# The experts' end of a decoder: results read back in portions by rank, summed in eight banks, normed in place

## The chip, the cores and the metric

The program is a small two-layer decoder in one kernel on one core of a Trainium2 chip. The metric is device time in microseconds (us), the median of the runs of one comparison. For the kernel before these are 3485.11 us, the median of three runs (3482.16 to 3487.38).

## The reference

The decoder runs three blocks twice, each with a residual and a layer norm. Only the last block matters here, a mixture of 64 experts with 8 of them for each of 2048 rows:

```python
x = _layernorm(x + _L1_ffn_ref(x, gate_w, w_gate, w_up, w_down), axis=-1)      # last line of the model
# inside _L1_ffn_ref: E = 64 experts, TOP_K = 8, HIDDEN = 256, FFN = 96, C = 2*N*8/64 = 512 slots an expert
scores, idx = top_k(softmax(x @ gate_w.T), 8)
xbuf = zeros((E, C, D)).at[e_sorted, pos].set(x[tok_sorted], mode='drop')
y = einsum('ecf,edf->ecd', silu(g) * u, w_down)
y_pair = y[e_sorted, safe_pos] * (s_sorted * valid)
out = zeros((N, D)).at[tok_sorted].add(y_pair)
```

So every output row is the row itself plus eight results of experts, each times its weight, and then a layer norm over 256 values.

## The kernel before

The stages run one after the other; the last is `stage_moe`. Its first part (`stage_cross`) writes each row to the slots of its experts in the DRAM table `xbuf` and keeps in `rows.row` (SBUF) the row itself, and a running count by which an expert knows its rank within a row's eight. Ranks go by expert number: rank 0 is the chosen expert with the lowest number, rank 7 the one with the highest. The second part, which the change touches, is the one block under `m = Mem(nc, ctx, "exp")`.

**The loop over pairs.** `PAIRS` is 32: two experts a pair, `i` from 0 to 31. SP loads the slots of both (`inputs`, L1442, three pairs deep) and the weights (`upper` L1377, `lower` L1382). PE turns the rows over (L1489), multiplies for gate (L1503) and up (L1507), and for the results `y` (L1520). ACT copies half of the turned rows (L1542), computes silu (L1553) and copies the results out of PSUM into the arena (L1563). DVE copies the other half (L1592), makes the addresses `cur` (L1596) and the products `h` (L1610, L1613). In every second pair, `i % 2`, DVE also makes the eight weights of one tile of 128 rows: three operations (L1621, L1624, L1627), 16 tiles in all. GpSimd (POOL) sends the results: four indirect DMAs an expert (L1662), 256 in all, each scattering up to 128 rows of 1 KB to `ytok` in DRAM, where row r and rank k lie at row 8r + k. Empty slots are skipped. After the sends of an expert it waits until those of the third expert back have landed, and frees their buffers.

**The end.** When all sends have landed, SP loads the results by tile: `load(t)` (L1465) brings all eight ranks of 128 rows, 8 KB in one piece for each partition, 1 MB a tile, into one of seven slots. Six slots lie in the arena that held inputs and results of the loop. Further loads wait until a slot is free. For each tile DVE adds ranks 0 and 1 times their weights to the row (L1641, `SCALED = 2`); ACT makes six diagonal matrices (L1571) and PE multiplies ranks 2 to 7 by them into one PSUM bank of four (L1533); DVE adds the bank (L1648) and takes mean and variance (L76, L79, L80); POOL makes the reciprocal root and the shift (L87, L90, L1676); ACT writes the normed tile into one of four buffers `out` (L1583); SP stores it (L1476). `RING = 4` buffers of each kind go round, so that diagonals wait for sums, sums for norms, and ACT's output for the store of four tiles before. Loads and stores are on SP's one queue, in the order in which they are issued.

Of the kernel before, what the change touches and what calls it, by code (L numbers as in the profile page):

```python
# [14 lines left out]
ALU = mybir.AluOpType  # L15
# [3 lines left out]
P = 128  # L19
# [1338 lines left out]
def stage_moe(nc, xc, dst, hold, qd, kd, xbuf, ytok, A):  # L1358
# [6 lines left out]
    with ExitStack() as outer:  # L1365
# [27 lines left out]
        with ExitStack() as ctx:  # L1393
# [3 lines left out]
            SLOTS, RING, SCALED = 7, 4, 2  # L1397
            TURNED = K - SCALED
            XG, Y, LOAD = QB * WIDTH, QB * D, K * D
# [7 lines left out]
            spare = m.sb("spare", [P, K, D])  # L1407
            yg = [cut(u * LOAD, LOAD, D) for u in range(SLOTS - 1)] + [spare[:, :, :]]
            part, out = ([m.sb(f"{n}{u}", [P, D]) for u in range(RING)] for n in ("part", "out"))
            diag = [m.sb(f"diag{u}", [P, TURNED, P]) for u in range(RING)]  # L1410
            power, eps = m.sb("power", [P, 1]), m.sb("eps", [P, 1])
            waiter, var, rstd, shift = ([m.sb(f"{n}{u}", [P, 1]) for u in range(RING)] for n in ("waiter", "var", "rstd", "shift"))
            st, mv = [m.sb(f"st{u}", [P, 6]) for u in range(RING)], [m.sb(f"mv{u}", [P, 2]) for u in range(RING)]
# [4 lines left out]
            same, same_w = m.sb("same", [P, K, E]), m.sb("same_w", [P, K, E])  # L1418
# [12 lines left out]
            y_in, stored, summed = m.sems("y_in", SLOTS), m.sems("stored", RING), m.sems("summed", RING)  # L1431
            diag_ready, sum_filled, shift_ready, norm_consts = m.sem("diag_ready"), m.sem("sum_filled"), m.sem("shift_ready"), m.sem("norm_consts")
            ln = [NormSems(m, u) for u in range(RING)]

            Mem.clear(nc)
            with nc.Block() as block:
                @block.sync
                def _(sp):
# [21 lines left out]
                    for b in range(RESULTS):  # L1460
                        for s in S:
                            sp.wait_ge(sent[b][s], len(range(b, PAIRS, RESULTS)) * QB * 16)

                    def load(t):
                        sp.dma_start(yg[t % SLOTS], results[:, t, :, :]).then_inc(y_in[t % SLOTS], 16)  # L1465

                    for t in range(SLOTS):
                        load(t)
                    for t in range(TILES + 2):
                        if t + SLOTS < TILES:  # L1470
                            sp.wait_ge(ln[t % RING].r, t // RING + 1)
                            load(t + SLOTS)
                        if t >= 2:
                            u = (t - 2) % RING
                            sp.wait_ge(ln[u].out, (t - 2) // RING + 1)
                            sp.dma_start(dst[(t - 2) * P:(t - 1) * P, :], out[u][:, :]).then_inc(stored[u], 16)  # L1476
                    for u in range(RING):
                        sp.wait_ge(stored[u], len(range(u, TILES, RING)) * 16)

                @block.tensor  # L1480
                def _(pe):
# [12 lines left out]
                    for i in range(PAIRS):  # L1494
# [18 lines left out]
                        for s in S:  # L1513
                            pe.wait_ge(h_ready[s], i + 1)
                            pe.wait_ge(late_ready[s], i + 1)
                            if i + 1 < PAIRS:
                                pe.wait_ge(x0_ready[s], i + 2)
                                pe.wait_ge(x1_ready[s], i + 2)
                            for b in range(QB):
                                last = pe.matmul(pxy[s][b // 2][:, b % 2 * D:b % 2 * D + D], h[s][:, b * P:b * P + P], wd[i % 2][s][:, :],  # L1520
                                                 start=True, stop=True)
                            last.then_inc(y_filled[s], 1)
                    for t in range(TILES):
                        u = t % RING
                        total = pxy[u // 2][u % 2]
                        pe.wait_ge(diag_ready, t + 1)
                        if t < RING:
                            pe.wait_ge(y_ready[u // 2], PAIRS)
                        else:
                            pe.wait_ge(ln[u].r, t // RING)  # L1530
                        pe.wait_ge(y_in[t % SLOTS], t // SLOTS * 16 + 16)
                        for k in range(TURNED):
                            last = pe.matmul(total[:, 0:D], diag[u][:, k, :], yg[t % SLOTS][:, SCALED + k, :], start=k == 0, stop=k == TURNED - 1)  # L1533
                        last.then_inc(sum_filled, 1)

                @block.scalar
                def _(act):
                    def half(i, s):
                        act.wait_ge(x_filled[s], i + 1)
                        if i:  # L1540
                            act.wait_ge(u_filled, i)
                        act.copy(xgT[s][:, 1, :], pxy[s][1][:, :]).then_inc(x1_ready[s], 1)  # L1542

                    for s in S:
                        half(0, s)
                    for i in range(PAIRS):
# [19 lines left out]
                    def diagonals(t):  # L1566
                        act.wait_ge(weight_ready, t + 1)
                        if t >= RING:
                            act.wait_ge(sum_filled, t - RING + 1)
                        for k in range(TURNED):  # L1570
                            last = act.mul(diag[t % RING][:, k, :], ident[:, :], weight[:, t, SCALED + k:SCALED + k + 1])  # L1571
                        last.then_inc(diag_ready, 1)

                    for t in range(RING):
                        diagonals(t)
                    for t in range(TILES):
                        u = t % RING
                        if t + RING < TILES:
                            diagonals(t + RING)
                        act.wait_ge(shift_ready, t + 1)  # L1580
                        if t // RING * 16 > 0:
                            act.wait_ge(stored[u], t // RING * 16)
                        act.activation(out[u][:, :], part[u][:, :], ACT.Identity, bias=shift[u][:, :], scale=rstd[u][:, :])\  # L1583
                           .then_inc(ln[u].out, 1)

                @block.vector
                def _(dve):
# [15 lines left out]
                    for i in range(PAIRS):  # L1603
# [12 lines left out]
                        if i % 2:  # L1616
                            t, done = i // 2, i // 2
# [6 lines left out]
                            dve.tensor_tensor(same_w[:, :, :], same[:, :, :], rows.weight[:, t:t + 1, :].broadcast_to([P, K, E]), ALU.mult)\  # L1624
                               .then_inc(same_w_ready, 1)
                            dve.wait_ge(same_w_ready, done + 1)
                            dve.tensor_reduce(weight[:, t, :], same_w[:, :, :], AX.X, ALU.add).then_inc(weight_ready, 1)  # L1627

                    dve.wait_ge(weight_ready, TILES)
                    for first in range(0, TILES, 2):  # L1630
                        tiles = first, first + 1
                        for k in range(SCALED):
                            for t in tiles:
                                u, turn = t % RING, t // RING
                                if k:
                                    dve.wait_ge(summed[u], turn * SCALED + k)
                                else:
                                    dve.wait_ge(y_in[t % SLOTS], t // SLOTS * 16 + 16)
                                    if turn > 0:
                                        dve.wait_ge(ln[u].out, turn)  # L1640
                                dve.scalar_tensor_tensor(out=part[u][:, :], in0=yg[t % SLOTS][:, k, :], scalar=weight[:, t, k:k + 1],  # L1641
                                                         in1=part[u][:, :] if k else rows.row[:, t, 0:D], op0=ALU.mult, op1=ALU.add)\
                                   .then_inc(summed[u], 1)
                        for t in tiles:
                            u, turn = t % RING, t // RING
                            dve.wait_ge(sum_filled, t + 1)
                            dve.wait_ge(summed[u], turn * SCALED + SCALED)
                            dve.tensor_tensor(part[u][:, :], part[u][:, :], pxy[u // 2][u % 2][:, 0:D], ALU.add).then_inc(ln[u].r, 1)  # L1648
                        for t in tiles:
                            u = t % RING  # L1650
                            norm_stats(dve, ln[u], [part[u][:, :]], [st[u][:, :]], [mv[u][:, :]], waiter[u], t // RING, 1)

                @block.gpsimd
                def _(pool):
# [15 lines left out]
                    for t in range(TILES):  # L1670
                        u = t % RING
                        if t >= RING:
                            pool.wait_ge(ln[u].out, t // RING)
                        norm_rstd(pool, ln[u], [mv[u][:, :]], [var[u][:, :]], eps[:, :], power[:, :], [rstd[u][:, :]], t // RING, 1)
                        pool.wait_ge(ln[u].rstd, t // RING + 1)
                        pool.tensor_scalar(shift[u][:, :], mv[u][:, 0:1], rstd[u][:, 0:1], -1.0, ALU.mult, ALU.mult).then_inc(shift_ready, 1)  # L1676
# [1301 lines left out]
```

## Time and profile before

| | |
|---|---|
| runs | 3485.11, 3487.38, 3482.16 us (median 3485.11) |
| profiled execution | 3484.81 us, of which the trace's span is 3483.1 us |
| mean granted TensorE clock | 0.968 of full speed |
| busy share of the span | PE 93%, weight loads 65%, DVE 68%, ACT 56%, POOL 59% |
| HBM read and written | 162.39 MB and 125.83 MB |

Times in rows are microseconds from the start of the span, unless marked ns. "Idle before" is how long the engine had nothing to do before the instruction, and the name behind the arrow is what ended that. A clock of 1.00 is 2.4 GHz, 0.50 is 1.2 GHz. The DMA share is the mean busy share of the core's 16 DMA engines.

### The profile page before, as it was taken

The page shows a single profiled execution, that of the slowest core. Times are in us where ns is not written, and L with a number is a line of the kernel's source. Part 1 is how long each engine was busy: PE and PEld are TensorE (multiplying, and loading weights), DVE is VectorE, ACT ScalarE, POOL GpSimd, SP SyncE. Part 2 cuts the span into 40 slices and gives each one's busy share as a digit, 9 for nine tenths or more (in the row PEclk, how much of TensorE's full clock was granted, in tenths as well). Part 3 has the DMA queues.
Part 4 walks back from the last instruction along what each step waited for, and adds up shares of the span by engine and source line. Part 5 has one row for each costly group of instructions (what it writes and reads, how often), then busy time and mean ns, then how long its engine had stood idle before and what let it go on. Part 6 is the DMA issues. An engine that isn't in the chain of part 4 may idle for free. (4 is left out here: it accounts for less than half of the span.)

```text
span 3483.1 us, 96172 instructions
## 1 busy us (share of the span) xinstructions
PE 3252.1 (93%) x37284; PEld 2271.6 (65%) x37284; DVE 2369.0 (68%) x4702; ACT 1952.6 (56%) x5231; POOL 2061.5 (59%) x3037
## 2 busy tenths in 40 slices
PE   9999899887899999999999999999999899699996
PEld 6777566465577777777777777777776455356665
DVE  5555477434677878787777878787777688444443
ACT  1111366422577677666777677767776477445555
POOL 3333477642566666666666666666666467657774
PEclk9999799997899999999999999999999899899998
DMA  2000555001111111111111111111210466266655
GB/s 86 17 11 12 134 130 121 30 1 25 53 55 58 46 51 51 52 43 52 49 52 55 40 51 54 52 43 51 60 40 21 109 162 173 104 224 209 213 181 232
DMA packets 222970, 278.87 MB, mean 80 GB/s; under 512 B 58420, under 2 KB 187000, under 8 KB 215832
## 3 DMA queue, kind: packets, MB, share of 16 engines
q1 hardware_dynamic: 201212, 236.71, 24.0%
q0 software_dynamic: 18432, 34.96, 2.9%
q8 instruction: 300, 4.92, 0.6%
q10 hardware_dynamic: 2876, 1.06, 0.1%
q14 instruction: 150, 1.23, 0.1%
HBM read 162.39 MB, written 125.83 MB: 83 GB/s over the span
## 5 line engine op out<-in xcount | busy, mean ns | idle before, releaser
L2333 PE MATMUL head_ring<-gd_xT,head_w 128*128 128x512 f32 x1024 | 508.6, 620 | 9.2 <-DMA head_w<-gd_w 6.8
L1662 POOL DMA_INDIRECT ytok<-exp_arena,exp_cur x256 | 251.0, 981 | 118.0 <-issue 73.5
L2661 DVE TENSOR_TENSOR head_Xs<-head_bx,head_join 128x512 bf16<-128x512 f32 x320 | 219.9, 687 | 80.9 <-PE head_bx L2375 80.9
L2333 PEld LDWEIGHTS head_ring<-gd_xT,head_w 128*128 128x128 f32 x1024 | 175.5, 191 | 148.6 <-issue 135.4
L2626 DVE SCALAR_TENSOR_TENSOR head_cb_V<-head_ring,head_taps,head_cb_V 128x504 f32<-128x504 f32 (+2 forms) x384 | 263.1, 727 | 2.8 <-ACT head_cb_V L2488 2.8
L2458 PE MATMUL head_by<-head_wo,head_ogT 128*128 128x256 f32 x1016 | 254.0, 393 | 7.0 <-issue 0.3
L2342 PE MATMUL head_ring<-head_w,gd_xT 128*128 128x256 f32 x1024 | 258.6, 396 | 0.0
L2458 PEld LDWEIGHTS head_by<-head_wo,head_ogT 128*128 128x128 f32 x1016 | 183.2, 190 | 37.3 <-DVE rows_xc L2694 13.7
L2342 PEld LDWEIGHTS head_ring<-head_w,gd_xT 128*128 128x128 f32 x1024 | 186.0, 191 | 32.4 <-issue 0.3
L2533 ACT CAST head_Tt<-head_btt 128x512 bf16<-128x512 f32 x320 | 194.3, 607 | 17.7 <-PE head_btt L2383 15.9
L2553 ACT COPY head_U<-head_bu 128x512 f32<-128x512 f32 x256 | 137.4, 589 | 109.8 <-PE head_bu L2421 109.8
L2626 DVE SCALAR_TENSOR_TENSOR head_cb_Q<-head_ring,head_taps,head_cb_Q 128x504 f32<-128x504 f32 (+2 forms) x192 | 141.0, 734 | 60.2 <-ACT head_cb_Q L2488 55.6
L1224 DVE TENSOR_REDUCE cf_top<-cf_near 128x4 f32<-128x1024 f32 x128 | 154.9, 1220 | 33.0 <-PE cf_near L1054 32.8
L2666 DVE TENSOR_TENSOR head_rest<-head_V,head_br 128x512 bf16<-128x512 f32 x128 | 88.0, 688 | 123.0 <-PE head_by L2439 117.9
L2530 ACT CAST head_Ti<-head_bx 128x512 bf16<-128x512 f32 x256 | 152.2, 595 | 34.2 <-PE head_bx L2293 34.2
L1146 ACT ACTIVATE cf_prob<-cf_score 128x512 f32<-128x512 f32 x256 | 145.7, 601 | 40.4 <-PE cf_score L1068 37.4
L749 ACT ACTIVATE cb_prob<-cb_score 128x384 f32<-128x384 f32 x256 | 121.6, 491 | 65.8 <-PE cb_score L682 63.5
L1610 DVE TENSOR_TENSOR exp_h<-exp_pgu,exp_act_g 32x512 f32<-32x512 f32 x64 | 44.2, 690 | 166.0 <-ACT exp_act_g L1553 166.0
L2560 ACT ACTIVATE head_o<-head_bu 128x128 f32<-128x128 f32 x512 | 137.5, 299 | 33.3 <-PE head_bu L2439 33.3
L1354 POOL DMA_INDIRECT xbuf<-moe_row,cf_to x128 | 127.0, 992 | 46.3 <-issue 38.7
L2755 POOL TENSOR_TENSOR head_knrm<-head_sums,gd_eps 128x4 f32<-128x4 f32 x64 | 13.3, 208 | 237.3 <-ACT head_kq L2516 237.3
L309 PE MATMUL la_bank<-la_xT,hold_place 128*128 128x256 f32 x640 | 149.1, 388 | 3.0 <-ACT la_xT L367 2.0
(389 smaller groups left out, 9342.9 us busy)
## 6 DMA issues: line engine op xcount, KB each, us to landing
xbuf<-head_blank SPq DMA_DIRECT2D x64, 552.0 KB
exp_arena<-xbuf SPq DMA_DIRECT2D x64, 552.0 KB, 5.2
hold_place<-scan SPq DMA_DIRECT2D x64, 256.0 KB, 4.6
ytok<-head_blank SPq DMA_DIRECT2D x64, 256.0 KB
exp_arena<-ytok SPq DMA_DIRECT2D x14, 1024.0 KB, 12.4
moe_w<-moe_w SPq DMA_DIRECT2D x32, 384.0 KB, 3.1
hold_place<-qd SPq DMA_DIRECT2D x48, 192.0 KB
hold_place<-kd SPq DMA_DIRECT2D x48, 192.0 KB
```

The costliest lines, as they stand in the source:

```text
L309: last = pe.matmul(b[:, j * N:j * N + N], wqk[:, c, h * DH:h * DH + DH], xT[u][:, c, :], start=c == 0, stop=c == DC - 1)
L1146: act.activation(prob[n % RING][:, :, :].rearrange("p i k -> p (i k)"), score[n % 2][:, :], ACT.Exp, scale=SCALE)\
L1224: dve.tensor_reduce(top[t % 2][:, :, j:j + 3:2].rearrange("p i j -> p j i"), near[n // 2 % 2][:, :].rearrange("p (a i k) -> p a i k", a=2, ...
L1662: pool.indirect_dma_start(ytok, bass.IndirectOffsetOnAxis(ap=cur[i % AHEAD][s][:, b:b + 1], axis=0), y[i % RESULTS][s][:, b, :], None, bou ...
L2333: last = pe.matmul(b[:, :], w[:, c, FEAT[what]], xT[:, c, n % UNITS * N:n % UNITS * N + N], start=c == 0, stop=c == DC - 1)
L2342: last = pe.matmul(b[:, i * D:i * D + D], xT[:, c, rows], w[:, c, FEAT["Z"]], start=c == 0, stop=c == DC - 1)
L2458: last = pe.matmul(bank[:, i * D:i * D + D], ogT[:, i, 2 * h + f, :], wo[:, h, :], start=h == 0, stop=h == REP - 1)
L2530: act.copy(Ti[:, :, :].rearrange("p q i -> p (q i)"), bt[:, :]).then_inc(t_ready, 1)
L2533: act.copy(Tt[:, :, :].rearrange("p q i -> p (q i)"), btt[:, :]).then_inc(tt_ready, 1)
L2560: last = act.activation(o2[:, v, block * P:block * P + P], bu[v][:, block * P:block * P + P], ACT.Square, accum_out=oss[:, v, block:block ...
L2626: dve.scalar_tensor_tensor(out=out, in0=by_seq(bank_of(f, n))[:, :, 0:SEQ - s], scalar=taps[:, TAP[f], KS - 1 - s:KS - s], in1=out, op0=AL ...
L2661: dve.tensor_tensor((Ti if a == 0 else Xs)[:, :, :], bx[:, :].rearrange("p (q i) -> p q i", i=SEQ), join[:, a, :].unsqueeze(1).broadcast_t ...
```

## The change

All of it is in the second part of `stage_moe`; the loop's matmuls, copies and sends are left as they are.

1. The results are read back in four portions by rank: portion g holds ranks 2g and 2g + 1 of all 16 tiles, 4 MB, in pieces of 2 KB (2 KB out of each 8 KB). SP issues portion g when the sends of pair 28 + g have landed (`results_sent` also waits for the two pairs before). Portion 0 lies in `hold.place`, portion 1 in `xc`, portion 2 in the arena (it also waits until the last inputs and addresses are read), portion 3 again in `hold.place`, for which it waits until DVE has added ranks 0 and 1 of all tiles. Portions 0 and 1 are two DMAs each, portion 2 four, portion 3 eight (one for two tiles).
2. DVE makes the weights of one tile in each pair from 1 to 16, in place in `hold.place`.
3. All 80 diagonals have a place of their own. ACT makes three of them in each pair from the fifth on, between its copies of turned rows and of results.
4. DVE adds ranks 0, 1 and 2, straight into `rows.row`, rank after rank over all 16 tiles. PE sums ranks 3 to 7 in eight banks, two tiles a bank: first rank 3 of all tiles, then ranks 4 and 5 of tiles 0 to 7, then for each bank ranks 6 and 7, with ranks 4 and 5 of tiles 8 to 15 in between.
5. Bank by bank DVE adds the sum and takes the statistics of two tiles, POOL makes roots for both at once, ACT norms `rows.row` in place, and SP stores from there. No buffer is waited for.

```diff
-            SLOTS, RING, SCALED = 7, 4, 2
+            ALONE = 3
+            TURNED, HALF = K - ALONE, K // 4
+            yg = [[hold.place[:, t * LOAD:t * LOAD + LOAD] for t in range(TILES)], [xc[:, t, :, :].rearrange("p k d -> p (k d)") for t in range(TILES)],
+                  [arena[:, t * LOAD:t * LOAD + LOAD] for t in range(TILES)],
+                  [hold.place[:, t * LOAD:t * LOAD + LOAD] for t in range(TILES)]]
+            diag = m.sb("diag", [P, TILES * TURNED, P])
+            totals = [m.ps("total"), pgu[0], pgu[1], pu, pxy[0][0], pxy[0][1], pxy[1][0], pxy[1][1]]
...
-                    for t in range(SLOTS):
-                        load(t)
-                    for t in range(TILES + 2):
-                        if t + SLOTS < TILES:
-                            sp.wait_ge(ln[t % RING].r, t // RING + 1)
-                            load(t + SLOTS)
+                    def results_sent(pair):
+                        for i in range(pair, -1, -1)[:RESULTS]:
+                            for s in S:
+                                sp.wait_ge(sent[i % RESULTS][s], (i // RESULTS + 1) * QB * 16)
+                    sp.wait_ge(weight_ready, TILES)
+                    for g in range(len(LOADS)):
+                        results_sent(PAIRS - len(LOADS) + g)
+                        if g == 2:
+                            for s in S:
+                                sp.wait_ge(x_filled[s], PAIRS)
+                                sp.wait_ge(cur_ready[s], PAIRS)
+                        if g == 3:
+                            sp.wait_ge(summed, 2 * TILES)
+                        for i, (first, last, to) in enumerate(LOADS[g]):
+                            sp.dma_start(to, results[:, first:last, g * HALF:g * HALF + HALF, :]).then_inc(y_in[g][i], 16)
+                    for t in range(TILES):
+                        sp.wait_ge(ln.out, t + 1)
+                        sp.dma_start(dst[t * P:t * P + P, :], row[t]).then_inc(stored, 16)
...
+                    def term(t, k):
+                        total = totals[t // 2][:, t % 2 * D:t % 2 * D + D]
+                        g = k // HALF
+                        pe.wait_ge(diag_ready, t * TURNED + k - ALONE + 1)
+                        pe.wait_ge(y_in[g][load_of(t, k)], 16)
+                        return pe.matmul(total, diag[:, t * TURNED + k - ALONE, :], value(t, k), ...)
+                    for t in range(TILES // 2):
+                        middle(t)
+                    for t in range(0, TILES, 2):
+                        for a in range(t, t + 2):
+                            for k in range(3 * HALF, K):
+                                last = term(a, k)
                         last.then_inc(sum_filled, 1)
+                        if t < TILES // 2:
+                            middle(TILES // 2 + t)
+                            middle(TILES // 2 + t + 1)
...
+                        diagonals((i - 4) * 3)
...
-                        if i % 2:
-                            t, done = i // 2, i // 2
+                        if 0 < i <= TILES:
+                            t, done = i - 1, i - 1
...
+                    for k in range(ALONE):
+                        for t in range(TILES):
+                            dve.scalar_tensor_tensor(out=row[t], in0=value(t, k), scalar=weight[:, t, k:k + 1], in1=row[t], op0=ALU.mult, op1=ALU.add)\
+                               .then_inc(summed, 1)
+                    for b in range(TILES // 2):
+                        tiles = 2 * b, 2 * b + 1
+                        dve.wait_ge(sum_filled, b + 1)
+                        for t in tiles:
+                            dve.tensor_tensor(row[t], row[t], totals[b][:, t % 2 * D:t % 2 * D + D], ALU.add).then_inc(ln.r, 1)
+                        norm_stats(dve, ln, [row[t] for t in tiles], [st[:, t, :] for t in tiles], [mv[:, t, :] for t in tiles],
+                                   waiter[:, 2 * b:2 * b + 2], b, 2)
```

## Rows read from the trace of the kernel before

**Rows 1.** Windows: start:end, length, busy time by engine, clock, DMA share, GB/s.

```profile
3165.00:3176.00 11.00, 10.89 (x48) 6.69 (x48) 6.36 (x12) 5.67 (x11) 7.92 (x9) 1.00 0.67 214
...
3420.00:3430.00 10.00, 3.13 (x8) 2.53 (x9) 1.27 (x3) 0.00 (x0) 0.40 (x1) 0.50 0.74 284
...
3440.00:3450.00 10.00, 10.00 (x48) 8.81 (x47) 6.33 (x24) 6.45 (x21) 5.33 (x12) 1.00 1.01 425
```

**Rows 2.** Chain that ended last, from 3419 us: start, length, what.

```profile
3419.42 2.28 DMA ytok<-exp_arena,exp_cur
...
3421.91 4.83 DMA exp_arena<-ytok
...
3445.68 13.21 DMA out<-exp_out
...
3476.28 0.60 ACT exp_out L1583
```

**Rows 3.** Timeline of GpSimd in the last pairs: sends of the results.

```profile
3388.94 0.97 POOL L1662 DMA_INDIRECT ytok<-exp_arena,exp_cur  x1 [0.94 <-ACT exp_arena L1563]
...
3397.89 0.97 POOL L1662 DMA_INDIRECT ytok<-exp_arena,exp_cur  x1 [0.30 <-issue]
...
3407.61 1.29 POOL L1662 DMA_INDIRECT ytok<-exp_arena,exp_cur  x1 [0.30 <-issue]
3409.20 0.97 POOL L1662 DMA_INDIRECT ytok<-exp_arena,exp_cur  x1 [0.31 <-ACT exp_arena L1563]
```

**Rows 4.** Timeline of DVE behind the last pair's matmuls.

```profile
3405.19 1.41 DVE L1613 TENSOR_TENSOR exp_h<-exp_pu,exp_act_g 64x512 f32<-64x512 f32 x2
...
3407.36 0.69 DVE L1624 TENSOR_TENSOR exp_same_w<-exp_same,moe_weight 128x512 f32<-128x512 f32 x1
```

**Rows 5.** DMA view from 3389 to 3409 us: the sends' queue, its share of 16 engines.

```profile
q0 software_dynamic: 674, 0.84, 12.0%
```

**Rows 6.** L1662's sends from 3200 to 3300 us, inputs loading beside them.

```profile
DMA to landing us min/median/max: 2.3/4.2/6.2
```

**Rows 7.** Windows of the kernel's start, when 2 KB pieces load; SP's issue, landing.

```profile
3.19 1.63 SPq L230 DMA_DIRECT2D hold_place<-wqT  x3
...
hold_place<-wqT SPq DMA_DIRECT2D x4, 512.0 KB, 6.9
...
8.00:10.00 2.00, 2.00 (x6) 1.55 (x5) 0.00 (x0) 0.00 (x0) 0.00 (x0) 1.00 1.06 404
10.00:12.00 2.00, 2.00 (x9) 1.63 (x8) 1.43 (x3) 0.00 (x0) 0.00 (x0) 1.00 1.06 388
...
20.00:22.00 2.00, 2.00 (x11) 1.77 (x10) 1.94 (x4) 0.00 (x0) 1.15 (x2) 1.00 1.01 324
```

**Rows 8.** Timeline of ACT, DVE and POOL inside the loop.

```profile
3387.10 1.07 ACT L1563 COPY exp_arena<-exp_pxy 128x512 f32<-128x512 f32 x2 [1.49 <-PE exp_pxy L1520]
3391.76 0.70 DVE L1610 TENSOR_TENSOR exp_h<-exp_pgu,exp_act_g 32x512 f32<-32x512 f32 x1 [3.16 <-ACT exp_act_g L1553]
3358.80 0.97 POOL L1662 DMA_INDIRECT ytok<-exp_arena,exp_cur  x1 [1.89 <-issue]
```

**Rows 9.** Timeline of the end: ACT's diagonals, PE's sums.

```profile
3410.66 7.12 ACT L1571 ACTIVATE exp_diag<-moe_ident,moe_share 128x128 f32<-128x128 f32 x24
...
3447.26 5.34 PE L1533 MATMUL exp_pxy<-exp_arena,exp_diag 128*128 128x256 f32 x24
```

**Rows 10.** Timeline of DVE for two tiles of the end.

```profile
3460.08 0.88 DVE L1641 SCALAR_TENSOR_TENSOR exp_part<-exp_arena,moe_share,exp_part 128x256 f32<-128x256 f32 x2
3460.87 0.76 DVE L1648 TENSOR_TENSOR exp_part<-exp_part,exp_pxy 128x256 f32<-128x256 f32 x2
...
3462.54 0.18 DVE L80 BATCH_NORM_AGGREGATE exp_mv<-exp_st 128x2 f32<-128x6 f32 x1
```

**Rows 11.** Timeline of POOL at the end: a root and a shift.

```profile
3475.33 0.55 POOL L90 TENSOR_TENSOR exp_rstd<-exp_var,exp_power 128x1 f32<-128x1 f32 x1
3475.98 0.27 POOL L1676 TENSOR_SCALAR exp_shift<-exp_mv,exp_rstd 128x1 f32<-128x1 f32 x1
```

More of the change, by code:

```diff
@@ L1406, in stage_moe, with by_tile, value, load_of @@
             y = [[cut(2 * INPUTS * XG + (2 * b + s) * Y, Y, D) for s in S] for b in range(RESULTS)]
[L1407 to L1410, printed above, removed]
+            assert TILES * LOAD <= 2 * INPUTS * XG + 2 * Y
+            def by_tile(flat):
+                return flat.rearrange("p (t k d) -> p t k d", k=HALF, d=D)
+            yg = [[hold.place[:, t * LOAD:t * LOAD + LOAD] for t in range(TILES)], [xc[:, t, :, :].rearrange("p k d -> p (k d)") for t in range(TILES)],
+                  [arena[:, t * LOAD:t * LOAD + LOAD] for t in range(TILES)],
+                  [hold.place[:, t * LOAD:t * LOAD + LOAD] for t in range(TILES)]]
+            LOADS = [[(0, 8, by_tile(hold.place[:, 0:8 * LOAD])), (8, TILES, by_tile(hold.place[:, 8 * LOAD:TILES * LOAD]))],
+                     [(0, 8, xc[:, 0:8, :, :]), (8, TILES, xc[:, 8:TILES, :, :])],
+                     [(t, t + 4, by_tile(arena[:, t * LOAD:t * LOAD + 4 * LOAD])) for t in range(0, TILES, 4)],
+                     [(t, t + 2, by_tile(hold.place[:, t * LOAD:t * LOAD + 2 * LOAD])) for t in range(0, TILES, 2)]]
+            def value(t, k):
+                return yg[k // HALF][t][:, k % HALF * D:k % HALF * D + D]
+            def load_of(t, k):
+                return next(i for i, (first, last, to) in enumerate(LOADS[k // HALF]) if first <= t < last)
+            row = [rows.row[:, t, 0:D] for t in range(TILES)]
+            diag = m.sb("diag", [P, TILES * TURNED, P])
             power, eps = m.sb("power", [P, 1]), m.sb("eps", [P, 1])
-            waiter, var, rstd, shift = ([m.sb(f"{n}{u}", [P, 1]) for u in range(RING)] for n in ("waiter", "var", "rstd", "shift"))
-            st, mv = [m.sb(f"st{u}", [P, 6]) for u in range(RING)], [m.sb(f"mv{u}", [P, 2]) for u in range(RING)]
+            waiter, var, rstd, shift = (m.sb(n, [P, TILES]) for n in ("waiter", "var", "rstd", "shift"))
+            st, mv = m.sb("st", [P, TILES, 6]), m.sb("mv", [P, TILES, 2])
             results = ytok.rearrange("(p t k) d -> p t k d", p=P, k=K)
@@ L1430, in stage_moe @@
             same_ready, same_w_ready, weight_ready = m.sem("same_ready"), m.sem("same_w_ready"), m.sem("weight_ready")
[L1431 removed]
+            y_in = [m.sems(f"y_in{g}", len(LOADS[g])) for g in range(len(LOADS))]
+            stored, summed = m.sem("stored"), m.sem("summed")
             diag_ready, sum_filled, shift_ready, norm_consts = m.sem("diag_ready"), m.sem("sum_filled"), m.sem("shift_ready"), m.sem("norm_consts")
[L1433 removed]
+            ln = NormSems(m, 0)
             Mem.clear(nc)
@@ L1459, in _ @@
                             lower(sp, i + 1)
[L1460 to L1465, printed above, removed]
-                    for t in range(SLOTS):
-                        load(t)
-                    for t in range(TILES + 2):
-                        if t + SLOTS < TILES:
-                            sp.wait_ge(ln[t % RING].r, t // RING + 1)
-                            load(t + SLOTS)
[L1473 to L1478, printed above, removed]
+                    def results_sent(pair):
[16 more added lines that the diff above has]
+                        sp.dma_start(dst[t * P:t * P + P, :], row[t]).then_inc(stored, 16)
+                    sp.wait_ge(stored, TILES * 16)
                 @block.tensor
@@ L1564, in _ @@
                             last.then_inc(y_ready[s], 1)
[L1566 to L1575, printed above, removed]
                     for t in range(TILES):
-                        u = t % RING
-                        if t + RING < TILES:
-                            diagonals(t + RING)
                         act.wait_ge(shift_ready, t + 1)
[L1581 to L1584, printed above, removed]
+                        act.activation(row[t], row[t], ACT.Identity, bias=shift[:, t:t + 1], scale=rstd[:, t:t + 1]).then_inc(ln.out, 1)
                 @block.vector
@@ L1629, in _ @@
                     dve.wait_ge(weight_ready, TILES)
[L1630 to L1643, printed above, removed]
-                        for t in tiles:
[L1645 to L1651, printed above, removed]
@@ L1669, in _ @@
                     pool.wait_ge(norm_consts, 1)
[L1670 to L1676, printed above, removed]
+                    for b in range(TILES // 2):
+                        two = slice(2 * b, 2 * b + 2)
+                        pool.wait_ge(ln.mv, 2 * b + 2)
+                        pool.tensor_tensor(var[:, two].unsqueeze(2), mv[:, two, 1:2], eps[:, :].unsqueeze(1).broadcast_to([P, 2, 1]), ALU.add).then_inc(ln.var, 1)
+                        pool.wait_ge(ln.var, b + 1)
+                        pool.tensor_tensor(rstd[:, two], var[:, two], power[:, :].broadcast_to([P, 2]), ALU.pow).then_inc(ln.rstd, 1)
+                        pool.wait_ge(ln.rstd, b + 1)
+                        for t in range(2 * b, 2 * b + 2):
+                            pool.tensor_scalar(shift[:, t:t + 1], mv[:, t, 0:1], rstd[:, t:t + 1], -1.0, ALU.mult, ALU.mult).then_inc(shift_ready, 1)
 class MlpWeights:
```

48 lines of the change are left out of this document (33 added, 15 removed).

## The prediction

> **What bounds the kernel now.** I read the windows first, then the chain that ended last, then the timeline of each engine from 3386 us on. In the loop over pairs the matmuls are the limit: in an 11.00 us window, one pair, PE is busy 10.89 us at full clock, the other engines 5.7 to 7.9 us and the DMA engines 0.67 of the time [rows 1]. Behind it the picture turns over. DVE's last products of the loop end at 3406.60 [rows 4]. The last send of results starts at 3419.42 and lands 2.28 us later, the first tile is issued at 3421.91 and lands after 4.83 us, at 3426.74, and the last norm on ACT starts at 3476.28 [rows 2]. From 3420 to 3430 PE has 3.13 us of work and its clock is down to 0.50, and from 3440 to 3450 the DMA engines are full, at 425 GB/s [rows 1]. The end is thus 77 us long (3406 to 3483), and its core is a read of 16 tiles of 1.05 MB: 16.8 MB at 425 GB/s, 39.5 us, none of which begins before 3421.91, though most results had landed long before. Around the core stands a ring: the chain goes through a store that took 13.21 us to land, being queued behind loads [rows 2], and the next output in that buffer waited for it.
>
> **1. Loads go out earlier (the gain).** I follow portion by portion, 4.19 MB each. A pair's sends: pair 29's run from 3388.94 to 3397.89, pair 30's begin at 3399.94 and its last is the one at 3409.20, pair 31's last is at 3419.42 [rows 2, 3]; pair 28's last is one slot of 1.28 us and a 0.94 us wait before 3388.94, at 3386.9. A send takes 2.28 us to land on idle engines [rows 2]; with inputs loading beside it the median is 4.2 and the worst 6.2 us [rows 6]. I take 3.3 us for pair 28 and 5 for the others, near the middle.
> The rate: the change reads 2 KB pieces, one of each 8 KB. The same shape is in the trace: the loads of wqT (1.5 MB in three of them, issued from 3.19 to 4.82) are 2 KB pieces 8 KB apart. They landed 6.9 us after issue in the median, so they moved in the stretch up to 12 us, where the rate was 404 and 388 GB/s [rows 7]. I take 395. The nearest bounds are 425 (8 KB pieces [rows 1]) and 324 (the end of woT's load, 1 KB pieces [rows 7]). The sends take 0.12 of the engines [rows 5], so beside them a portion takes 4.19 / (395 x 0.88) = 12.1 us, alone 10.6. From issue to landing there are 2.4 us besides the data (4.83 less 1.05 MB at 425 [rows 1, 2]).
> Portion 0: issued 3390.2, landed 3390.2 + 2.4 + 12.1 = 3404.7. Portion 1: issued at about 3402.9, landed 3417.4. Portion 2: issued at 3414.2, in line behind portion 1, landed 3429.1 (the sends thin out after 3424). Portion 3: issued when pair 31's sends have landed, 3419.4 + 1.5 (for item 2) + 4.5 = 3425.4, still in line: first eighth (two tiles, 1.3 us) at 3430.5, last at 3439.8. Before, by the same count, the reads alone ran to 3421.9 + 2.4 + 39.5 = 3463.8.
> The page DMA: Bandwidth & Descriptors of the Trainium skill (section Latency and other measured facts) states that copies whose rows lie at large powers of two lose rate, with a few channels of the HBM as the supposed reason; it starts at 512 KiB, while a partition's rows here lie 128 KB apart before and after. If the same held for 2 KB of each 8 KB, the read would slow; rows 7 show none of it.
>
> **2. DVE's first part.** 48 additions (ranks 0 to 2) instead of 32, with nothing to wait for but the loads. Two of them take 0.88 us and are 0.79 us apart in start from what follows [rows 10], so 0.40 each. DVE is free at 3406.6 (3405.19 + 1.41 [rows 4]), portion 0 is there: ranks 0 and 1 end at 3406.6 + 32 x 0.40 = 3419.4, before pair 31's sends land, so SP's new wait on them costs nothing; if they ran late, all of portion 3 and the stores are queued behind that wait on SP. Rank 2 ends at 3425.8, ahead of the first bank. But these additions run beside the last ten sends. The trace has one such meeting: a DVE operation with two operands in SBUF at 3407.36 [rows 4], and the send that began at 3407.61 took 1.29 instead of 0.97 us [rows 3]. Bounds: 0 and 11 x 0.32 = 3.5 us later; I take 1.5, a little under the middle, because that operation was 0.69 us long and these are 0.40 [rows 4, 10].
> The page SBUF — State Buffer of the Trainium skill (section Who interferes with whom) has this as a rule: a VectorE instruction with both inputs in SBUF shuts out a GpSimd instruction that reads SBUF. It speaks against the change. Taken strictly, each send would wait for an addition, which is the upper bound above.
>
> **3. PE.** Sum terms 80 instead of 96. 24 take 5.34 us, 0.225 each [rows 9]; each now has two waits of its own ahead of it, which no row prices: between 0 and 0.08 us (a third of a term), I take 0.025, so 0.25. Rank 3 and the first 16 of ranks 4 and 5 fit ahead of portion 3. Then PE's clock will be low: after idling it had 0.50, and then 8 terms took 3.13 us instead of 2.0 [rows 1]. Bank 0's four and its four in between: 3430.5 to 3433.6; banks 1 and 2 to 3437.6; bank 3's sum at 3438.6; banks 4 to 7 follow at 1 us each from 3440.6 to 3443.6.
>
> **4. DVE's second part, POOL, ACT, store.** From the adds of two tiles to the last statistics: 3460.87 to 3462.72, 1.85 us [rows 10]. Bank 0 is summed at 3432.1; up to bank 3 (3438.6) DVE waits for PE, then PE for nobody and DVE is last: 3438.6 + 5 x 1.85 = 3447.9. Behind it var, root and two shifts, 1.5 us (root to shift start is 0.65, a shift 0.27 [rows 11]), and one ACT norm with its start, 0.8: 3450.2. From there to the span's end before: 3483.1 - 3476.88 = 6.2 us (store and close [rows 2]). Sum: 3456.4. The ring's waits and the store behind loads are gone; what is late next is DVE.
>
> **5. Hidden edits.** Diagonals: 24 took 7.12 us [rows 9], so three cost 0.9 us of ACT in each pair, where it idles 1.49 us before the results' copy [rows 8]. If that cover were gone, the copy and with it the sends would move 0.9 us in 27 pairs, 24 us. Weights twice as often in pairs 1 to 16: 2.1 us of DVE in a pair where it idles 3.16 us with them in it [rows 8], in a pair of 11.00 us that is as long with them as without. Both at nothing. In the last pair they are gone from DVE, which frees 2.1 us.
>
> **The sum.** Span 3483.1 - 3456.4 = 26.7 us less. The profiled execution's own time was 1.7 us over its span, and the median 0.3 over that: 3456.4 + 2.0 = 3458.4, forecast 3458.
>
> **The rivals.**
> A, the forecast: the DMA engines, then DVE. 3453 to 3463. Chance 0.55.
> B, the sends are late. They share the engines with full queues, and POOL has under 1 us to spare in a pair (7.92 busy, eight sends of 1.28 in 11.00 [rows 1, 3]). Each slowed by 0.32, that is 3.5; landing at 6.2; and one stall of 1.89 us as at 3358.80 [rows 8] in each of the last two pairs, 3.8: portion 3 is issued at 3419.4 + 3.5 + 3.8 + 6.2 = 3432.9 instead of in line at 3426.7, and 6.2 us go on top: 3464.6. Chance 0.22. For it speaks the landing, against it that the sends skip empty slots and move 0.84 MB in 20 us [rows 5].
> C, the faster side: reads at 425 beside the sends (3.5 us less over four portions) and PE warm (1.1 less), DVE's banks at 1.7: 3453. Chance 0.13.
> D, slower than before: pieces of 2 KB, one in four, hit part of the memory at a time. The price is the rate: the end is the last landing plus about 16.6 us less what PE and DVE did meanwhile, at least 1 + 1.85 + 2.3 + 6.2 = 11.4. It decides when the last landing is at 3471.7, so (3471.7 - 3392.6) for 16.8 MB and 0.12 for the sends: below 16.8 / (79.1 x 0.94) = 226 GB/s. At 200 GB/s it would give 3493. Rows 7 speak against it, at 388 GB/s. The page's rule above is this rival. Chance 0.05.
> E, the change doesn't do what it says: SP's waits pass only at the end (a landed pair is seen late, or the sends starve until the portions before are in) and the reads run from 3421.9 at 395: 3421.9 + 2.4 + 42.5 + 11.4 + 2.0 = 3480. Nothing in the rows speaks for it but the shared engines. Chance 0.05.
>
> **Range and chances.** 3450 to 3471 takes in A, C's value and B with a further stall. Within 0.2% of the time before (about what a measurement can tell from no change) is 3478.1 to 3492.1. Faster 0.90, same 0.05 (E and the mild half of D), slower 0.05.
>
> **What would show it.** The windows from 3390 to 3440 at a DMA share near 1 with 340 to 400 GB/s; four groups of loads issued near 3390, 3403, 3414 and 3425; sends of 1.28 us spacing up to 3420 and the pairs still 11.00 us apart; DVE's 32 additions over by 3420; PE idle only before portion 3; eight groups of DVE 1.85 us apart at the end. Wrong are my steps if the loads' groups are late (B, E), if the share is 1 at a lower rate (D), or if PE's terms come at 0.3 us or more, which would put PE behind DVE as the last in line.

## The result: faster by 10.5 us, two fifths of what was forecast

The changed kernel took 3472.64 us in the median of seven runs (3464.95 to 3475.1), the kernel before 3483.14 us on the same chip: ratio 0.997, 95% interval 0.996 to 0.9979. The forecast was 3458, the range 3450 to 3471. On another chip, ten runs against thirteen, the ratio was 0.9979 (0.9967 to 0.9992). The sign was right, the size was not.

The profiled execution's span is 3473.4 us. These windows of the changed kernel answer to [rows 1]; the columns are the same.

```profile
3166.00:3177.00 11.00, 10.89 (x50) 6.70 (x49) 6.35 (x12) 6.56 (x14) 7.92 (x9) 1.00 0.65 207
...
3391.00:3401.00 10.00, 9.89 (x47) 6.22 (x46) 4.38 (x8) 5.52 (x11) 6.88 (x8) 1.00 0.98 352
...
3430.00:3440.00 10.00, 1.69 (x8) 1.14 (x6) 0.00 (x0) 0.00 (x0) 3.99 (x5) 0.71 0.36 116
3440.00:3450.00 10.00, 9.77 (x36) 8.33 (x37) 3.27 (x16) 1.09 (x2) 1.84 (x6) 0.78 1.01 373
3450.00:3460.00 10.00, 10.00 (x48) 8.83 (x47) 5.03 (x25) 3.28 (x6) 3.91 (x12) 1.00 0.23 76
```

The loop is untouched: a pair still takes 11.00 us with PE busy 10.89, and ACT's busy time rose from 5.67 to 6.56 us for the three diagonals. From 3391 to 3401, where the DMA engines had a share of 0.14 in the kernel before, they are full beside the loop. But from 3430 to 3440 almost nothing happens: PE 1.69 us, DVE none, DMA 0.36. And from 3450 to 3460 PE is busy without a pause while the DMA engines are mostly free.

SP's issues of the four portions, start and time of issuing:

```profile
3389.61 1.06 SPq L1495 DMA_DIRECT2D hold_place<-ytok  x2
3403.42 1.07 SPq L1495 DMA_DIRECT2D rows_xc<-ytok  x2
3414.76 4.41 SPq L1495 DMA_DIRECT2D exp_arena<-ytok  x4
3436.58 4.12 SPq L1495 DMA_DIRECT2D hold_place<-ytok  x8
```

Forecast were 3390.2, 3402.9, 3414.2 and 3425.4. Three are within 0.6 us, the fourth is 11.2 us late. GpSimd's timeline says why (to be read with [rows 3]), and DVE's, below it, says beside what:

```profile
3406.03 0.97 POOL L1695 DMA_INDIRECT ytok<-exp_arena,exp_cur  x1 [0.30 <-issue]
3407.31 1.15 POOL L1695 DMA_INDIRECT ytok<-exp_arena,exp_cur  x1 [0.30 <-issue]
3408.77 1.28 POOL L1695 DMA_INDIRECT ytok<-exp_arena,exp_cur  x1 [0.30 <-issue]
3410.35 15.92 POOL L1695 DMA_INDIRECT ytok<-exp_arena,exp_cur  x1 [0.30 <-issue]
3426.58 0.97 POOL L1695 DMA_INDIRECT ytok<-exp_arena,exp_cur  x1 [0.30 <-issue]
...
3434.24 0.97 POOL L1695 DMA_INDIRECT ytok<-exp_arena,exp_cur  x1 [0.30 <-issue]
```

```profile
3406.34 12.76 DVE L1673 SCALAR_TENSOR_TENSOR moe_row<-hold_place,moe_share,moe_row 128x256 f32<-128x256 f32 x32
3419.01 6.41 DVE L1673 SCALAR_TENSOR_TENSOR moe_row<-rows_xc,moe_share,moe_row 128x256 f32<-128x256 f32 x16
```

One send of 0.97 us lasted 15.92. It ended at 3426.27, 0.85 us behind DVE's last addition at 3425.42. It also ended just as portions 1 and 2 had all but come in (389 GB/s from 3426 to 3427 us, 198 in the next), so two causes fit: DVE's additions, or the full DMA queues.

The second loss is on PE. Its timeline from the landing of portion 3 on, which answers to the PE row of [rows 9]:

```profile
3445.86 1.89 PE L1550 MATMUL exp_pgu<-hold_place,exp_diag 128*128 128x256 f32 x8
3447.58 1.89 PE L1550 MATMUL exp_pxy<-exp_arena,exp_diag 128*128 128x256 f32 x8
...
3456.22 7.07 PE L1550 MATMUL exp_pxy<-hold_place,exp_diag 128*128 128x256 f32 x32
```

Four terms are a group of 8 instructions, and groups are 1.72 us apart: 0.43 us a term. The view counts two instructions for one of these matmuls. The prediction took the 24 of [rows 9] for 24 terms; they are 12, and the 8 of [rows 1] are 4.

### The profile page after: what moved, and what is told of

Same layout as the page of the kernel before. It is cut to its first block and busy times, and to the rows that moved or that the text cites. A ratio compares the mean times of both kernels' runs of the same rounds, so it can differ in the third digit from the quotient of the medians.

```text
span 3473.4 us, 96144 instructions
## 1 busy us (share of the span) xinstructions
PE 3245.1 (93%) x37252; PEld 2268.7 (65%) x37252; DVE 2372.7 (68%) x4718; ACT 1945.7 (56%) x5215; POOL 2070.3 (60%) x3021
## 5 line engine op out<-in xcount | busy, mean ns | idle before, releaser
L1695 POOL DMA_INDIRECT ytok<-exp_arena,exp_cur x256 | 266.6, 1041 | 117.6 <-issue 73.8
L2568 ACT CAST head_Tt<-head_btt 128x512 bf16<-128x512 f32 x320 | 194.0, 606 | 17.1 <-PE head_btt L2418 15.9
```

The source lines that it names most:

```text
L1695: pool.indirect_dma_start(ytok, bass.IndirectOffsetOnAxis(ap=cur[i % AHEAD][s][:, b:b + 1], axis=0), y[i % RESULTS][s][:, b, :], None, bou ...
L2568: act.copy(Tt[:, :, :].rearrange("p q i -> p (q i)"), btt[:, :]).then_inc(tt_ready, 1)
```

## The experiments

Theory L: DVE's row of additions, with two operands in SBUF each and no break, keeps GpSimd from reading its addresses. Theory Q: the full DMA queues hold the send. Theory P: behind portion 3, PE ends last; theory V: DVE or the loads do. The first four kernels ran together, once each, on a chip on which everything took longer (kernel before 3647.7 us, mean clock 0.951); their times are compared with that run alone, and the changed kernel itself was not run there.

**Additions after the sends.**

```diff
                     dve.wait_ge(weight_ready, TILES)
                     done = [0] * TILES
+                    for i in range(PAIRS - RESULTS, PAIRS):
+                        for s in S:
+                            dve.wait_ge(sent[i % RESULTS][s], (i // RESULTS + 1) * QB * 16)
```

> The changed kernel, but DVE begins its 48 additions only when the sends of the last pairs have landed. In the changed kernel one send lasted 15.92 us and ended 0.9 us behind DVE's last addition. Theory L (DVE's unbroken row of additions, two SBUF operands each, keeps GpSimd out of SBUF): all sends are about 0.97 us long and 1.28 us apart, the last starts near 3419; the additions run from about 3424, portion 3 waits for 32 of them and is issued near 3437, as late as before, so the span stays within 4 us of 3473. Theory Q (the queues filled by portions 1 and 2 hold the send back): a send of 14 to 16 us is there again, the additions start near 3436, portion 3 goes out near 3449 and the span is about 3486.

Measured 3635.64 us, 12.1 less than the kernel before. No send was longer than 0.98 us, though portion 1, and then portion 2, were in the queues beside them (DMA share 0.98 from 3560 to 3570 us); the last began at 3577.74. The additions ran from 3583.25 to 3596.01, and portion 3, which waits for them, went out at 3596.10, 49.4 us after portion 0 (47.0 in the changed kernel). As theory L had it, the loss only moved from the send to the wait; theory Q's long send is missing. The stretch from DVE's last products to the end is 69.0 us, 1.9 more than in the changed kernel.

**Loads after the sends.**

```diff
-                        results_sent(PAIRS - len(LOADS) + g)
+                        results_sent(PAIRS - len(LOADS) + g if g == 0 else PAIRS - 1)
```

> The changed kernel, but portions 1, 2 and 3 are all issued only when pair 31's sends have landed; portion 0 and the additions of ranks 0 and 1 stay where they are, so the additions run beside nearly idle DMA engines. Theory L: one send is held until the 32 additions are over, near 3419, so it lasts 9 to 10 us, the last send starts near 3428, the reads of 12.6 MB take 32 us more and the span is 3480 to 3488. Theory Q: no send is longer than 1.3 us, the last starts near 3419.5 and the span is 3472 to 3480.

Measured 3667.61 us, 19.9 more than the kernel before. A window, GpSimd's send and DVE's additions:

```profile
3588.00:3598.00 10.00, 0.00 (x0) 0.00 (x0) 9.54 (x25) 0.93 (x2) 10.00 (x1) 0.69 0.00 1
```

```profile
3587.98 10.41 POOL L1695 DMA_INDIRECT ytok<-exp_arena,exp_cur  x1 [1.82 <-issue]
3598.70 0.97 POOL L1695 DMA_INDIRECT ytok<-exp_arena,exp_cur  x1 [0.30 <-issue]
```

```profile
3584.79 12.76 DVE L1673 SCALAR_TENSOR_TENSOR moe_row<-hold_place,moe_share,moe_row 128x256 f32<-128x256 f32 x32
```

The DMA engines moved 1 GB/s, and the send still took 10.41 us. It ended at 3598.39, 0.84 us behind the last addition (3597.55). That is the same distance as in the changed kernel (0.85). Theory Q falls. The time is not as expected, though: 3 us less to 5 more than the kernel before was said, 19.9 more came. By the table below, 4.6 of them lie behind the first addition (81.1 against 76.5, the latter from another chip). The rest lies ahead of it: the additions began at 3584.79, while DVE was through with the loop at 3560.41 to 3564.94 in the three kernels beside this one. No run tells why.

**One operand instead of two.** Ranks 0 and 1 are left out of the result here.

```diff
+                            if k < HALF:
+                                dve.tensor_reduce(reduced[:, t * HALF + k:t * HALF + k + 1], value(t, k), AX.X, ALU.add).then_inc(summed, 1)
+                            else:
                                 dve.scalar_tensor_tensor(out=row[t], in0=value(t, k), ...)
```

> The changed kernel, but in place of the 32 additions of ranks 0 and 1 DVE takes sums over the same values (tensor_reduce: one SBUF operand, 128x256 read, one column written), so ranks 0 and 1 are left out of the result. DMA traffic and DVE's row of work without a break are the same. Theory L with the second operand as its cause: no send over 1.3 us, the last near 3419.5, portion 3 issued near 3425, span about 3462 to 3466. Theory L with any unbroken DVE work: the send of 10 us and more stays. Theory Q: it stays too.

Measured 3621.49 us, 26.2 less than the kernel before, where 17 to 21 less was expected (the stretch behind the loop, in the table below, is 19.4 shorter). DVE's work and a send beside it, with the loads running:

```profile
3562.56 10.54 DVE L1675 TENSOR_REDUCE exp_reduced<-hold_place 128x1 f32<-128x256 f32 x32
3573.02 1.66 DVE L1677 SCALAR_TENSOR_TENSOR moe_row<-rows_xc,moe_share,moe_row 128x256 f32<-128x256 f32 x4
3575.83 0.48 DVE L1677 SCALAR_TENSOR_TENSOR moe_row<-rows_xc,moe_share,moe_row 128x256 f32<-128x256 f32 x1 [1.15 <-issue]
...
3579.33 3.65 DVE L1677 SCALAR_TENSOR_TENSOR moe_row<-rows_xc,moe_share,moe_row 128x256 f32<-128x256 f32 x9 [0.90 <-DVE moe_row L1677]
```

```profile
3573.46 1.28 POOL L1699 DMA_INDIRECT ytok<-exp_arena,exp_cur  x1 [0.30 <-issue]
```

32 sums without a break left every send beside them at 0.97 us; the first longer one is that at 3573.46, which met the additions with two operands that follow. One of these began 1.15 us late; but another waited 0.90 us after the last send had ended (3577.29), so that a send holds back an addition in its turn is not shown. It is not DVE's being busy, then, that holds a send. A sum differs from an addition in more than the second operand, however: it writes one column instead of 256 and takes no weight. The kernel before has rows for both. Its copies write 128x512, and its operations L1621 and L1624 take two operands from SBUF and no weight:

```profile
3385.65 0.97 POOL L1662 DMA_INDIRECT ytok<-exp_arena,exp_cur  x1 [0.32 <-issue]
3386.93 1.07 POOL L1662 DMA_INDIRECT ytok<-exp_arena,exp_cur  x1 [0.31 <-issue]
```

```profile
3385.66 0.69 DVE L1592 COPY exp_xgT<-exp_pxy 128x512 f32<-128x512 f32 x1
...
3386.47 0.68 DVE L1621 TENSOR_TENSOR exp_same<-moe_row,moe_rank 128x512 f32<-128x512 uint8 x1
```

From 3149 us to the last send, 107 sends there met a copy or a product, which have at most one operand in SBUF, and none of them was over 0.98 us. 24 met L1621 or L1624, and nine of these took 1.07 to 1.29 us; no other send was over 0.98. (L1596 takes two operands from SBUF as well, of four values a partition, and lasts about 0.2 us; it lengthened none of the 35 sends that met it without the other two.) So it is the second operand from SBUF.

**A break behind each addition.**

```diff
                                .then_inc(summed, 1)
+                            dve.wait_ge(summed, count + 1)
```

> The changed kernel, but DVE waits after each addition until that addition has finished (its own semaphore) before it issues the next, so there is a short break between any two. Theory L in its strong form (a row without breaks is what keeps GpSimd out, a single addition costs at most 0.4 us): sends grow by 0 to 0.4 us each, the last starts before 3424, portion 3 goes out when the additions allow it, near 3427, span 3463 to 3467. If single additions are enough to shut GpSimd out: the send stays at 15 us or longer. Theory Q: it stays at about 16 us.

> The changed kernel with DVE waiting for each addition to finish before the next, timed. Theory L: no send over 1.3 us; portion 3 goes out 8 to 14 us earlier than in the changed kernel, and the time falls by as much: 8 to 14 us less than the changed kernel, 18 to 26 us less than the kernel before (ratio near 0.9935). Theory Q: the same time as the changed kernel within 3 us.

On the first chip 3619.43 us, 28.3 less than the kernel before, where 16 to 20 less was expected (the stretch is 19.2 shorter). Timed with the changed kernel on another chip: 3464.37 us (four runs) against 3474.26 (ten) and 3482.55 for the kernel before; ratio 0.994 (0.9921 to 0.9959). DVE, GpSimd and SP there:

```profile
3408.96 16.81 DVE L1673 SCALAR_TENSOR_TENSOR moe_row<-hold_place,moe_share,moe_row 128x256 f32<-128x256 f32 x32
```

```profile
3411.22 1.16 POOL L1696 DMA_INDIRECT ytok<-exp_arena,exp_cur  x1 [0.31 <-issue]
...
3421.90 1.07 POOL L1696 DMA_INDIRECT ytok<-exp_arena,exp_cur  x1 [0.30 <-issue]
```

```profile
3427.55 8.24 SPq L1495 DMA_DIRECT2D hold_place<-ytok  x8
```

The 32 additions cost 16.81 instead of 12.76 us, the sends next to nothing (at most 0.19 each). Portion 3 went out 18.6 us behind the first addition, in the changed kernel on this chip 30.3.

> The changed kernel itself, on the same chip as the next three, so that they have it to compare with. Theory L: again one send of 12 to 16 us that ends within 1.5 us of DVE's last addition, portion 3 issued 14 to 18 us later than with breaks between the additions; ratio to the kernel before 0.996 to 0.998.

The changed kernel itself, there: 3474.26 us. In its trace the send lasted 15.93 us, from 3407.19 to 3423.12, beside additions from 3403.18 to 3422.27: the same 0.85 us behind their end.

**A break behind every fourth addition** (the same wait under `if count % 4 == 3`).

> The changed kernel, but DVE waits for its own completion only after every fourth addition, so a row without a break is four additions, 1.6 us. Theory L (GpSimd gets in only at a break): single sends of up to 0.97 + 1.6 = 2.6 us, none of 10 us or more; from the start of the additions portion 3 goes out after 18 to 23 us (changed kernel 30.3, with a break after each addition 18.6). If the length of a row didn't matter (one break in four is as bad as none), a send would still last over 8 us.

Measured 3461.32 us in one run, beside 3482.34 for the kernel before. No send was longer than 1.15 us, and portion 3 went out 18.7 us behind the first addition, while the 32 additions took only 13.63 us. One break in four is enough. Sends of up to 2.6 us had been expected: the length of a row of four does not show in the sends.

**Ranks 4 and 5 of all tiles ahead of portion 3**, with and without breaks.

```diff
-                    for t in range(TILES // 2):
+                    for t in range(TILES):
                         middle(t)
...
-                        if t < TILES // 2:
-                            middle(TILES // 2 + t)
-                            middle(TILES // 2 + t + 1)
```

> The changed kernel, but PE sums ranks 4 and 5 of tiles 8 to 15 right behind those of tiles 0 to 7, before portion 3, instead of between the banks. A term costs two of the instructions that the views count, 0.43 us, so 16 terms are 6.9 us. Theory P (in the changed kernel PE is idle ahead of portion 3 because of the held send, and behind it PE is what ends last): the time falls by 5 to 7 us. Theory V (DVE's banks or the loads end last, as the prediction had it): it falls by less than 2 us.

> Both: breaks between the additions, and all of ranks 4 and 5 before portion 3. With the send free PE has hardly an idle stretch left ahead of portion 3, so theory P gives only 0 to 3 us less than breaks alone; if PE's terms were not the limit (theory V) it gives nothing or up to 2 us more. Against the kernel before: 19 to 28 us less.

> The kernel with a break behind each addition and with ranks 4 and 5 of all tiles before portion 3, again, beside the next one: 17 to 24 us less than the kernel before.

Without breaks 3464.82 us (ratio 0.9951, 0.9932 to 0.9969), 9.4 less than the changed kernel, more than the 5 to 7 expected. With breaks 3462.09 us (0.9936, 0.9917 to 0.9955), 2.3 less than breaks alone, and in the second comparison 3461.24 us (0.9931, 0.9915 to 0.9948): the fastest of the timed kernels, 21 us under the one before. Since the point at which the end begins moves between executions, I also read from each trace the stretch from DVE's first addition to the end of the span, in us ("before" and "additions after": from where DVE is through with the loop's products). "First chip" is the one with 3647.7 us:

| kernel | from | span | stretch |
|---|---|---|---|
| before | 3406.63 | 3483.1 | 76.5 |
| changed | 3406.34 | 3473.4 | 67.1 |
| changed, other chip | 3403.18 | 3470.4 | 67.2 |
| breaks | 3408.96 | 3467.8 | 58.8 |
| break every fourth | 3399.26 | 3459.6 | 60.3 |
| middle first | 3401.95 | 3460.5 | 58.5 |
| both | 3404.84 | 3461.5 | 56.7 |
| both, again | 3402.20 | 3460.8 | 58.6 |
| four ranks on DVE (below) | 3407.33 | 3466.0 | 58.7 |
| additions after, first chip | 3564.94 | 3633.9 | 69.0 |
| loads after, first chip | 3584.79 | 3665.9 | 81.1 |
| one operand, first chip | 3562.56 | 3619.7 | 57.1 |
| breaks, first chip | 3560.41 | 3617.7 | 57.3 |

Moving 16 terms out of the stretch behind portion 3 gives 8.7 us where PE had been idle ahead of it, and 0 to 2 us where it had not. Theory V (under 2 us without breaks) is out. That 8.7 is more than the 6.9 us of the 16 terms has to do with PE's clock: behind 10.21 us of idleness portion 3's first 8 instructions took 3.75 us at a clock of 0.50 (changed, other chip), behind 1.89 us 1.97 at 1.00 (middle first). "Break every fourth" is 1.5 us longer than "breaks" for the same reason: 3.65 us at 0.50 for these 8 instructions against 1.97 at 1.00. PE of "both", the last group before and the first behind portion 3's landing:

```profile
3430.51 7.07 PE L1550 MATMUL exp_pxy<-exp_arena,exp_diag 128*128 128x256 f32 x32
3437.41 1.89 PE L1550 MATMUL exp_total<-hold_place,exp_diag 128*128 128x256 f32 x8
```

No gap is left between them. PE waited last for the second half of portion 1, 0.22 us up to 3420.06, and works without a gap from there on; the bound is then PE's work, from the second half of rank 3's terms to the last.

**Four ranks on DVE, 64 terms on PE** (`ALONE = 4`, breaks in the first 32 additions, middle first).

> As that kernel, but DVE adds four ranks instead of three (64 additions, breaks only in the first 32) and PE sums four (64 terms of 0.43 us instead of 80). Theory P (from the landing of portion 2 on PE works without a pause on the 64 terms of ranks 4 to 7, so rank 3 was ahead of that and cost nothing): 0 to 3 us less. If PE's 80 terms as a whole were the limit, 6 to 7 us less. If DVE is then the last, 0 to 3 us more.

Measured 3467.77 us (five runs) against 3461.24 of the kernel it is compared with: 6.5 more, which none of the three cases had. The stretch, though, is 58.7 us, as long as that kernel's 58.6. The difference stands in the traces already where the loop over pairs begins. PE's gate matmuls of the same pair in this kernel and in "both, again":

```profile
3070.26 3.60 PE L1524 MATMUL exp_pgu<-exp_xgT,moe_w 128*128 128x512 f32 x8
```

```profile
3065.11 3.60 PE L1524 MATMUL exp_pgu<-exp_xgT,moe_w 128*128 128x512 f32 x8
```

From there to the end of the loop it is 337.0 to 337.1 us in all nine traces outside the first chip, the kernel before among them. So the starts in the table, 3399 to 3409, scatter by the stages ahead of the loop, in whose code no edit changes anything; why they took 5 us longer in this kernel's trace is open. Behind the loop PE idles 15.38 us ahead of portion 2:

```profile
3425.74 2.05 PE L1550 MATMUL exp_total<-exp_arena,exp_diag 128*128 128x256 f32 x4 [15.38 <-DMA exp_arena<-ytok]
```

```profile
3425.00:3427.00 2.00, 1.26 (x3) 1.11 (x4) 2.00 (x7) 0.00 (x0) 0.00 (x0) 0.50 1.05 407
```

Without rank 3 it came to portion 2 18.4 us behind the first addition instead of 20.8 ("both, again"), but then took 30.2 us to its last term instead of 27.8: its first instructions ran at a clock of 0.50, and it waited once more, 0.59 us, for a piece of portion 2. So taking rank 3 off PE gained nothing, but not because rank 3 had been ahead of the bound, as theory P had it: PE came to its work 2.3 us earlier and lost them to the clock and the wait. That PE's 80 terms as a whole were the limit, at 6 to 7 us less, is out.

## Why the prediction was wrong

**Step 1, the loads, held.** Three issue times within 0.6 us; beside the sends 352 GB/s at a DMA share of 0.98, alone up to 406 GB/s, where I had 348 and 395. The 2 KB pieces are as fast as wqT's. Rival D had nothing for it, nor had E. The sends landed after 5.7 us in the median, 5 had been taken.

**Step 2 failed, in the price of a send beside DVE.** I had the right contact, the rows for it and the rule, and priced each meeting by one row: 0.32 us for a send that met one operation [rows 3, 4], eleven times, 3.5 us at most, 1.5 taken. What the step overlooked is that in the kernel before a send met at most two such operations in a row (L1621, L1624); here 48 follow each other. The send that was shut out did not get in between two additions but only when DVE stopped: 14.95 us for one send. The seven behind it followed 1.28 us apart, the last at 3434.24 instead of near 3420.9, and landed in 2.3 us instead of 4.5. Portion 3 went out at 3436.58 instead of 3425.4, and its first eighth was used at 3440.24 instead of 3430.5: 9.7 us. The Trainium skill, on the page SBUF — State Buffer (section Who interferes with whom), calls the pair of ports that DVE shares with GpSimd an exclusive lock, and says that a DVE instruction with two SBUF inputs contends with a GpSimd instruction that reads SBUF. The runs agree, and go further: with one operand no send was held, with two the hold outlasted some 37 whole instructions (15.07 us at 0.40). Rival B had the late sends, by other mechanisms (landing, stalls of GpSimd), and its 3464.6 was too low.

**Step 3 failed, in the cost of a term.** 0.25 us stood for 0.43, from counting two instructions as two terms. A check was at hand: the view groups 168 + 24 instructions at L1533 for 16 tiles of 6 terms, which is two for each. From the first term of portion 3 to the last bank I had 13.1 us (3430.5 to 3443.6); measured are 23.1 (3440.24 to 3463.30), 10.0 more. The waits ahead of each term cost nothing that shows: 0.43 us a term against 0.445 before. The slow clock behind the idle stretch was there as said: the first 8 instructions took 3.75 us instead of 1.89. "PE's terms at 0.3 us or more", which the prediction names as a sign of being wrong, is what came.

**Step 4 held in its prices, not in its place.** A group of DVE takes 1.64 us (3458.14 to 3459.78; 1.85 taken), and the last four are 1.73 apart, which is PE's pace; the tail from DVE's last statistics to the end 8.4 us (8.5 taken). But DVE waits 1.8 us for PE in each of the first banks, and ends 1.7 us behind PE instead of 4.3, which gives 2.6 us back. Together: 9.7 + 10.0 - 2.6 = 17.1, and the span was 17.0 us over the forecast (3473.4 against 3456.4).

**Step 5 held.** Diagonals and weights cost the loop nothing: from the same pair's gate matmuls to DVE's last products it is 337.1 us in the trace before and in the changed one.

With the breaks the same plan gives 18 us of gain instead of 8 on one chip. By the stretch, 58.8 us against the 49.8 that I had forecast (3406.6 to 3456.4), 9.0 remain. PE's terms are 7.9 of them (21.0 us from portion 3's first term to the last, 13.1 forecast), 3.9 are that portion 3 is used 27.8 us behind the first addition instead of 23.9, and DVE's ending closer behind PE gives 2.6 back.

## What to carry to other kernels

A DVE operation with two SBUF operands beside GpSimd's indirect DMAs should be priced by the length of the row it stands in, not by one meeting; one wait of DVE for its own result after every fourth of 32 additions lengthened them by 0.9 us here, and the stretch behind the loop fell from 67.2 to 60.3. Before a count of a view is multiplied, it should be divided by what the code says the count is. When loads are drawn ahead under a loop, as here, look at what the last portion's release hangs on, and leave as little work as possible behind it.

## What the runs showed of the hardware

A GpSimd send that met an unbroken row of DVE's two-operand additions was held until the row ended: 15.92 and 15.93 us in two traces of the changed kernel, 15.93 with the middle first, 10.41 with the loads after the sends. Each ended 0.84 to 0.85 us behind the last addition. In the changed kernel two sends before it got through within the same row with 0.18 and 0.31 us lost; why the third did not, no run tells. A break of about 0.13 us behind each addition (4.05 us over 32) was enough to let the sends in, and so was a break behind every fourth. Beside DVE operations with at most one operand in SBUF no send was over 0.98 us. Reads of 2 KB out of each 8 KB moved at 352 to 406 GB/s.
